# Who begins five loads of each head: the sync queue or ScalarE, in an attention and mixture kernel

## The reference

```python
x = x + gamma * attention(layernorm(x), ctx, ctx)
x = x + mixture(layernorm(x), U, V, W1, b1, W2, b2)
```

## Time and profile before

| what | value |
|---|---|
| median of 3 runs | 1733.92 us (1733.26 to 1735.15) |
| the profiled execution's own time | 1722.16 us |
| its span, first to last instruction | 1720.3 us |
| granted TensorE clock, mean | 0.992 |
| busy share of the span | PE 91%, DVE 58%, ACT 44%, POOL 42% |
| DMA, 16 engines, whole span | 171 GB/s |

### The profile page before, as it was taken

How to read it: one execution, slowest core, us unless ns; L and a number is a source line. 1 busy time by engine, 2 the same in 40 slices (tenths; PEclk the granted TensorE clock), 3 DMA queues, 4 the chain that set the end, 5 groups by cost and what they waited for, 6 DMA issues and landing times.

```text
span 1720.3 us, 22223 instructions
## 1 busy us (share of the span) xinstructions
PE 1567.6 (91%) x6496; PEld 1158.5 (67%) x6496; DVE 993.3 (58%) x1290; ACT 764.7 (44%) x1222; POOL 715.5 (42%) x523
## 2 busy tenths in 40 slices
PE   5988888898888888888975999999999999999999
PEld 3656565565655666665653777787878778787877
DVE  7788788888788877878872643332323233332312
ACT  5666667676666766666653411212121221212120
POOL 3778778787777878787852000000000000000000
PEclk9999999999999999999997999999999999999999
DMA  5889898988889888888877312040212112030202
GB/s 175 253 258 284 244 284 248 281 268 265 271 255 282 251 282 243 283 254 272 258 241 225 111 58 90 9 138 0 98 49 80 66 41 105 0 112 34 98 1 74
DMA packets 128155, 294.22 MB, mean 171 GB/s; under 512 B 34432, under 2 KB 39552, under 8 KB 128128
## 3 DMA queue, kind: packets, MB, share of 16 engines
q1 hardware_dynamic: 128128, 293.87, 54.7%
HBM read 125.87 MB, written 33.69 MB: 93 GB/s over the span
## 4 chain that ended last, share of the span: by engine, by line
PE 47%; SPq 39%; issue 6%; DMA 5%; DVE 1%; POOL 1%; ACT 1%; ACTq 0%; POOLq 0%
SPq L223 32%; PE scores L928 20%; PE scores L971 10%; PE attended L989 10%; PE spare L1008 2%; DMA gains<-gain 2%; DMA x_res<-in_x 1%; SPq L234 1%; DMA pt<-pb 1%; SPq L239 1%; SPq L229 1%; PE scores L943 1%; PE scores L946 1%; SPq L201 1%; SPq L215 1%
## 5 line engine op out<-in xcount | busy, mean ns | idle before, releaser
L342 POOL TENSOR_TENSOR pt_lo<-pt,pt_hi 128x512 fp32r<-128x512 f32 (+1 forms) x256 | 399.4, 1561 | 173.9 <-ACT pt_hi L411 173.3
L418 ACT ACTIVATE probs<-scores,neg_max 128x1024 f32<-128x1024 f32 x256 | 284.5, 1111 | 205.7 <-DVE neg_max L571 205.5
L571 DVE TENSOR_REDUCE neg_max<-scores 128x1 f32<-128x1024 f32 x256 | 311.8, 1218 | 104.2 <-PE scores L517 103.5
L580 DVE STREAM_TRANSPOSE pb<-probs 128x1024 f32<-128x1024 f32 x256 | 316.3, 1236 | 43.7 <-DMA pt<-pb 43.6
L853 POOL TENSOR_TENSOR rstd<-var_eps,minus_half 128x1 f32<-128x1 f32 x28 | 17.2, 614 | 609.3 <-DVE var_eps L1054 609.3
L517 PE MATMUL scores<-k_hi,q_hi 128*128 128x512 f32 x512 | 236.6, 543 | 23.2 <-ACT probs L418 14.0
L539 PE MATMUL attended<-pt_hi,v_hi 128*128 128x512 f32 x320 | 140.5, 439 | 123.5 <-POOL pt_lo L342 123.4
L411 ACT ACTIVATE pt_hi<-pt 128x512 fp32r<-128x512 f32 (+1 forms) x256 | 186.6, 729 | 93.9 <-DMA pt<-pb 86.1
L928 PE MATMUL scores<-nt_hi,w_hi 128*128 128x512 f32 x512 | 200.8, 392 | 2.5 <-DVE w_lo L1079 2.5
L872 ACT ACTIVATE hidden<-scores,b_col 128x512 f32<-128x512 f32 x64 | 44.2, 690 | 351.0 <-PE scores L928 351.0
L928 PE MATMUL scores<-nt_lo,w_hi 128*128 128x512 f32 x512 | 200.2, 391 | 0.0
(11 more groups left out here) (95 smaller groups left out, 2640.5 us busy)
## 6 DMA issues: line engine op xcount, KB each, us to landing
pt<-pb SPq DMA_DIRECT2D x1024, 128.0 KB, 2.7
x_raw<-in_x SPq DMA_DIRECT2D x32, 512.0 KB, 7.2
k_raw<-in_ctx SPq DMA_DIRECT2D x32, 512.0 KB, 4.8
gain_row<-gains SPq DMA_DIRECT2D x64, 256.0 KB, 4.4
x_res<-in_x SPq DMA_DIRECT2D x32, 512.0 KB, 6.9
x<-x_out SPq DMA_DIRECT2D x64, 256.0 KB, 4.5
first_n<-x SPq DMA_DIRECT2D x32, 512.0 KB, 3.5
result<-x SPq DMA_DIRECT2D x64, 256.0 KB, 3.7
```

The lines of the kernel that those rows point to most:

```text
L342: nc.gpsimd.tensor_tensor(pt_lo[2 * parity + half][:, :, keys, :], pt[2 * parity + half][:, :, keys, :], as_f32(hi[half][q][:]), ALU.subtr ...
L418: nc.scalar.activation(probs[j % 2][:], scores[j % 2][:], ACT.Exp, bias=neg_max[:, j:j + 1], accum_out=row_sum[b][:, j:j + 1]).then_inc(s_ ...
L571: nc.vector.tensor_reduce(neg_max[:, j:j + 1], scores[j % 2][:], AX_X, ALU.max, negate=True).then_inc(s_max, 1)
L580: nc.vector.transpose(pb[half][:, :, j % HALF, :], probs[j % 2][:]).then_inc(s_blocks, 1)
```

## The change

Five kinds of load of each head leave SP's slot and are begun by ACT, with the same data, sizes, tiles and semaphores: `v_nat` of h in block 2, k of h+2 in block 3, x of h+2 in block 4, `v_raw` of h+1 and the residual of h-1 in block 5. Each stands behind the `pt_hi` activation (and, in block 2, behind the rounding of the values) of its block. The waits that guarded the loads move with them; SP keeps its wait on `s_pv`, and ACT waits in addition on `s_added` ahead of the residual's load. The loads ahead of head 0 stay with SP, which also loads `v_nat` of head 0 there. The residual of the last head stays with SP.

```diff
@@ sync, slot
             if last:
                 load_first(n)
-            if more:
-                sp.wait_ge(s_klo, h + 2)
-                load_k(h + 2)
             if not (known and h < 2):
                 sp.wait_ge(s_pv, n - JB)
-            load_v_native(h, parity)
-            if not last:
-                sp.wait_ge(s_vlo, h + 1)
-                load_v(h + 1)
             if not first:
                 spread_gain(h - 1, 0)
             if not first:
                 send_gain(h - 1, 1)
             if not (known and h < 2):
                 store_x1(h - 2, 1)
-            if not first:
-                load_residual(h - 1)
-            if more:
-                sp.wait_ge(s_q32, h + 2)
-                load_x(h + 2)
             gather(h, n, 0, parity)
@@ sync, ahead of the slots
         load_k(1)
+        load_v_native(0, 0)
         h, n = over_heads(sp, slot)
@@ scalar (load_x, load_k, load_v, load_v_native and load_residual as in sync, with act.dma_start)
         def slot(h, n, parity, first, last):
+            known = isinstance(h, int)
+            more = not (known and h + 2 >= heads)
...
                 if j == 2:
                     high_values(h, n, parity)
+                    if not first:
+                        load_v_native(h, parity)
+                if j == 3 and more:
+                    act.wait_ge(s_klo, h + 2)
+                    load_k(h + 2)
+                if j == 4 and more:
+                    act.wait_ge(s_q32, h + 2)
+                    load_x(h + 2)
+                if j == 5 and not last:
+                    act.wait_ge(s_vlo, h + 1)
+                    load_v(h + 1)
+                if j == 5 and not first:
+                    if not (known and h < 2):
+                        act.wait_ge(s_added, h * 2 - 2)
+                    load_residual(h - 1)
                 if j == 3 and not last:
                     queries(h + 1, 1 - parity)
```

More of the change, by code:

```diff
@@ L401, in scalar, with rows_of @@
     def scalar(act):
+        def rows_of(h):
+            return bass.ts(h, P)
         def high_probs(quarter):
@@ L412, in high_probs, with load_x, load_k, load_v @@
                                  ACT.Copy).then_inc(s_pthi, 1)
+        def load_x(h):
+            act.dma_start(x_raw[:], x[rows_of(h), :]).then_inc(s_x_in, 16)
+        def load_k(h):
+            act.dma_start(k_raw[:], ctx[rows_of(h), :]).then_inc(s_k_in, 16)
+        def load_v(h):
+            act.dma_start(v_raw[:, 0:SPLIT, :], ctx_t[rows_of(h), 0:SPLIT * P].rearrange("p (b d) -> p b d", d=P)
+                         ).then_inc(s_v_in, 16)
+        def load_v_native(h, parity):
+            act.dma_start(v_nat[parity][:], ctx_t[rows_of(h), SPLIT * P:].rearrange("p (b d) -> p b d", d=P)
+                         ).then_inc(s_vn_in, 16)
+        def load_residual(h):
+            act.dma_start(x_res[:], x[rows_of(h), :]).then_inc(s_res_in, 16)
         def exps(s, j, b):
```

## The result

The changed kernel took 1718.03 us in the median of 4 runs (1714.08 to 1720.17) where the kernel before took 1734.54 (1733.26 to 1739.51, 4 runs): a ratio of 0.990, 95% interval 0.987 to 0.993. Timed again later it gave 0.991 (0.988 to 0.994). So it is about 16 us faster, where 28 us were forecast (1706). The direction and the range held; a bit over half of the gain came.

What follows compares the result with a forecast made beforehand. SP's order of issuing gathers was taken to bound each 27.58 us head; weighing SP's cycle (26.6) against the engines' bound (26.65) gave 0.93 us less a head, 28 us over some 30 heads: 1706 us, range 1692 to 1726.

Steps and rivals of the forecast that it cites:

- the ring and its two terms: Block 0 to next block 0: 15.12 us until half 0's gathers start, 12.53 until they land; only the first can shrink.
- the price on ACT: Five loads issued by ACT under running activations: cost taken as nothing, high end 0.62 us each.
- what is freed behind the reading back: SP's slot between the gain row's reading back and half 0's gathers: residual and x gone, 0.94 + 0.15 us gained.
- up to that much can be added to the row's landing, or nothing. I take 0.5 us.: k's 512 KB under way when the first gain row is sent: landing later by 0 to 1.8 us, 0.5 taken.
- The sum: Per head: SP's gather cycle 26.6 us, engines' bound 26.65; 26.65 taken, a gain of 0.93 us in some 30 heads.
- my signs of being wrong: Second sending later than 13.5 us after block 0, gathers landing over 2.5 us after last issue, or residual over 9 us.
- The rival in which ACT is held: k's 0.62 us issue delays block 4's gain; heads take 27.0 us or a little more, 1716 us; chance 0.08.
- the residual: Residual's load beside the gathers lands about 1.0 us later; 0.7 us passes to PE and DVE, bound 25.96 to 26.65.
- the larger of two limits: A head's length taken as the larger of SP's gather cycle, 26.6 us, and the engines' bound, 26.65 us.
- The transfers' volume: Rival: half 0's landing hangs on transfer volume, not issue time, so the head stays; 1734 us; chance 0.07.
- The starved residual: Rival: residual lands over 2.0 us later, about 9 us after issue, holding POOL in block 7; 1746 us; chance 0.10.

Runs made afterwards that it cites:

- the first ten rows of the table: The kernel before (ratio 1), the changed kernel timed twice (0.990, 0.991), and seven edits of the changed kernel to k's load, the first gain row's sending or the residual (0.975 to 0.994).
- row and residual repaired: Changed kernel with the first gain row sent after 8 of the 16 gathers of half 1 and the residual loaded in block 4: ratio 0.975.
- k beside the train: Changed kernel with k's load in block 6, beside the gathers of half 0, and the residual in block 4: ratio 0.986.
- the spread row late: Kernel before with only the residual and x begun by ACT; k, v_nat and v_raw stay with SP: ratio 0.998.
- sendings stand inside the train: Two kernels sending both gain rows after 8 gathers: the kernel before (0.990), and the changed kernel with second store likewise, residual in block 4, k in block 6 (0.973).
- the last kernel: Changed kernel with both gain rows and the second store sent after 8 gathers, residual in block 4, x in block 5, k in block 6: 0.973, 1685.52 us.
- the residual first: Changed kernel with residual and x exchanged on ACT, the residual in block 4 and x last in block 5: ratio 0.994.
- The small k: Changed kernel with ACT's load of k cut from 1024 to 32 columns (16 KB instead of 512 KB), issue, wait and semaphore kept: ratio 0.983.
- k back with SP: Changed kernel with k alone given back to SP, behind the first gain row and the store: ratio 0.986.

## Why the prediction was right or wrong

**Right: the ring and its two terms.** The head's length is the start of the gathers of half 0 plus 12.5 to 12.8 us in the first ten rows of the table, from before (27.58 - 15.05 = 12.53) to row and residual repaired (26.47 - 13.69 = 12.78). That part of the working carried the experiments. Below those rows the term grows: to 13.1 with k beside the train, to 13.2 with the spread row late, to 13.0 and 14.9 where sendings stand inside the train. In the last kernel the train starts as soon as DVE allows, takes 11.7 us to issue and lands 3.1 us later.

**Right: the price on ACT.** Nothing was taken, with 0.62 us a load as the other end. ACT issued in 0.34 us under running activations. The gain stayed at 12.44 us after block 0 in the heads shown; its mean rose from 12.45 to 12.65, and was 12.45 again with the residual first and all five loads on ACT.

**Right: what is freed behind the reading back.** 0.94 + 0.15 = 1.09 us were counted; the stretch from the reading back to the gathers shrank by 1.29 us in the heads shown (2.86 to 1.57), and by 1.27 in the mean.

**Wrong, and this is the step that failed: "up to that much can be added to the row's landing, or nothing. I take 0.5 us."** It was k's 512 KB beside the first gain row. The mean landing went from 2.55 to 4.18 us, 1.6 us more, close to the 1.8 that I had as the upper end. SP's arrival had been just in time in every second head; now it waited in all. The second sending moved from 12.84 to 13.94 us after block 0, which ate 1.1 of the 1.2 us that the residual and x had freed. The small k (0.983) and k back with SP (0.986) show it, each from another side. I chose 0.5 between bounds with no row near either, and overlooked that k would put back the tail of the train ahead of the row: 2.2 us from the end of the last issue to the last landing became 3.8 (40.10 against 36.31 after block 0). That is the row's whole delay: it landed 0.7 us behind the last gather before and 0.6 in the changed kernel, and 0.45 to 0.7 in the mean of each of the ten traces in which it is sent behind the train.

**Held in part by luck: the number.** The sum put a head at 26.65 us; the two traces of the changed kernel have 27.48 and 27.41, 0.1 to 0.2 us less than before instead of 0.93, that is 3 to 5 us in all. The median lies in the range because the timed runs differ by 16 us, most of which the heads in the traces don't show. One of my signs of being wrong was met: the second sending came 13.94 us after block 0, beyond 13.5. The gathers of half 0 started at 14.95, not at 13.8 to 14.4. The other two signs stayed away (2.2 us from the last issue to the landing of half 0; 7.5 us for the residual). The rival in which ACT is held gave 1716, nearer to the measured 1718 than my 1706, though what it describes didn't happen.

**Right in direction, and hidden: the residual.** About 1.0 us later was the estimate; the median landing went from 6.9 to 7.5 us, and POOL's wait, without the longest, from 18.1 us in 18 heads to 46.9 in 28, that is to 1.7 us each, where I had said nearer 2. DVE was ready for the next block 0 at 26.46 us in the mean, before at 26.12, where I had put 26.65 and 25.96. The residual's lateness cost nothing in the changed kernel, where the row was the later of the two, and 0.5 to 1.2% once the row was repaired. To forecast by the larger of two limits was the right form; the ring, which I put at 26.6, was the larger, 27.48 us against 26.46.

**The rivals.** ACT was not held. The transfers' volume didn't set the end: the best kernel moves the same bytes in 47 us less. The starved residual did not decide; its median landing of 7.5 us stayed below the 9 where it would have. By the rule of the Trainium skill ("DMA: Bandwidth & Descriptors", "Issuing engines are not separate DMA queues"), only the sequencer's issue time is saved by issuing from several engines. These runs don't follow it by itself: k back with SP costs SP an issue more and is faster (0.986 against 0.990 and 0.991), because the move also changes which transfer is under way ahead of which. What the Trainium skill says of turns between queues (the same page, "Queues, rings and completion order") is neither shown nor refuted: k costs the row 1.6 us from ACT's queue, where it begins 1.9 us before the row is sent, and 0.1 us from SP's, where it begins 1.3 us behind it, so that queue and moment changed together.

**What stays open.** Why the runs show 16 us and the profiled pair 2 is settled in part. The granted clock was 0.992 in the profiled execution of before and 0.987 in the mean of the 39 timed runs of that kernel beside the experiments, and among these the time falls as the clock rises (1741.60 us at 0.980, 1724.34 at 0.992). The changed kernel's ten runs had 0.991 and 1716.8 us in the mean; a line through the 39 puts the kernel before at 1728.7 us there. By that estimate some 12 us belong to the change at an equal clock, 3 to 5 of which the heads show; whether the change also raises the granted clock isn't known. That x, begun at 491.40 in the head shown, adds to the row's landing wasn't tried by itself; it is issued as the row lands, so it can hardly.

## What to carry to other kernels

Ask of a moved load not only what its issue costs where it goes, but which small transfer someone is waiting for while its data run: here 512 KB of k cost a gain only as long as SP stood waiting for a row of 2 KB behind them, and were harmless in the same place once it didn't. Where a queue must wait for a round trip, send the first leg inside the bulk work before it, so that the landing is mostly hidden (SP's wait for it fell from 100.9 us to 13.0). And of two causes that stand one behind the other, repairing one may bring little or nothing (0.986 to 0.988 and 0.994 here, against 0.975 together): repair both before judging either.

## What the runs showed of the hardware that I had not expected

A DMA of 2 KB that lands in 2.55 us behind a train in its own queue takes 4.18 us when 512 KB were begun on another queue 1.9 us before it. It is the train's tail that is late: the last of 16 gathers of 128 KB lands 3.8 us after its issue instead of 2.2, and the row lands 0.45 to 0.7 us behind it in the mean of each of the ten traces with that order. A DMA that ACT begins while it computes costs its arithmetic nothing that the trace can show: it takes 0.34 us of ACT's instruction stream, and with all five loads on ACT and the residual first the exponentials of block 4 start 11.08 us after block 0 in the mean, before 11.07. And the issue of a gather of 32 rows of 4 KB takes 0.59 us in a train where a load of 128 rows takes 0.35.
